# The bias of the last two token tiles moved to ScalarE and GpSimd, and a shorter chain to the integers, in an attention and int8 feed-forward kernel

## The chip, the cores and the metric

The kernel runs on 8 cores of one Trainium2 chip. Each core takes one batch entry (2048 tokens of 1024 features), and nothing passes between cores. The time is device microseconds of the slowest core for one execution. TensorE (PE) multiplies, VectorE (DVE), ScalarE (ACT) and GpSimd (POOL) do the elementwise work, SyncE (SP) issues most of the stores.

## What is computed

```python
s = einsum('bhqd,bhkd->bhqk', q * d**-0.5, k)
attn = where(causal, 1 + s + 0.5*s*s, 0)
o = einsum('bhqk,bhkd->bhqd', attn, v) / (sum(attn) + 1e-6)
x = layernorm(x + (o @ Wo.T))
x_scale = maximum(max|x|, 1e-6) / 127            # per token
x_q = clip(round(x / x_scale), -128, 127)         # int8
y = (x_q @ weight_q.T) * x_scale * weight_scale + bias
out = layernorm(x + y)
```

16 heads of 64; all inputs are float32 but for the int8 weight. The change concerns the lines from the first layernorm to `bias`, for the last 256 of a core's 2048 tokens.

## The kernel before

A core works its 2048 tokens as 16 tiles of 128 tokens (one token per partition). Five attention groups run one after another; projections, output projections and the feed-forward of earlier tiles are woven between the attention's matmuls by a planner in Python (`drive`, with a clock in `at` and `when_idle`). Tiles 0 to 13 pass wholly through that stream. The last two, tiles 14 and 15, form the end of the program (from L1020 on), whose order is written out by hand and which the change alone touches.

Each engine has one queue of instructions, filled in the order in which the helpers are called; an instruction waits for semaphores that other engines raise, and all that is queued behind it on its engine waits too. In the end part `V` puts an instruction on VectorE and `A` one on ScalarE. The order of calls, at the bottom of the function, is:

```python
scales(ta, sums(ta)); tx = sums(tb); turned(ta); hold(4)
scales(tb, tx); biased(ta); forward(ta); turned(tb)
added(ta, 0); added(ta, 1); biased(tb); forward(tb)
tv = spread(ta); added(tb, 0); last_norm(ta, tv)
added(tb, 1); last_norm(tb, spread(tb))
```

with `ta` tile 14 and `tb` tile 15. What each does:

- `sums(t)`: the residual and its sum on VectorE in two halves of 512 columns (L1057), then the sum of squares on ScalarE (L1059).
- `scales(t)`: largest and smallest value (L1068, L1073), the mean and 1/sigma, then a chain of 128x1 VectorE operations, each of which waits for the one before. L1074 and L1075 make the largest deviation `d`, L1077 its scaled form `xs_`, L1078 multiplies `xs_` by 1/127, L1079 takes the reciprocal, L1080 multiplies it by 1/sigma (`s2`), L1081 makes the offset `mm2`. With these ScalarE writes one half of the integers (L1083) and VectorE the other (L1085). A magic constant in float16 rounds them. The stored `xs_` (scale `XS`) is read again by `added`.
- `turned(t)`: eight transposes on TensorE (L1095), copied out of PSUM by ScalarE (L1101) and VectorE (L1104).
- `biased(t)`: x times 1/sigma plus the bias row, 128x1024, one VectorE instruction (L1111). Writing back to the tile's buffer, it waits only for ScalarE's half of the integers.
- `forward(t)`: 16 matmuls of 512 columns into two PSUM banks (L1118).
- `added(t, half)`: VectorE scales one bank (L1129), adds it to the biased x and sums (L1132, which waits for `biased(t)`); ScalarE squares the half and sums (L1136).
- `spread(t)`: mean and variance, on VectorE (L1142, L1143, L1144; L1143 waits for both squares) and a root on ScalarE (L1145).
- `last_norm(t)`: 1/sigma and offset (L1150, L1151), the output in two halves by ScalarE (L1152) and VectorE (L1156), each stored by SyncE.

Elsewhere, L669 is the only other tensor instruction of GpSimd: the division of attention outputs by their sums. L902 is VectorE's final normalization of tiles 0 to 13, and L605 VectorE's first step on the last attention group, after an L669.

Of the kernel before, what the change touches and what calls it, by code (L numbers as in the profile page):

```python
# [10 lines left out]
AF = mybir.ActivationFunctionType  # L11
ALU = mybir.AluOpType
# [24 lines left out]
INV127 = 1.0 / 127.0  # L37
# [80 lines left out]
def build_nc():  # L118
# [17 lines left out]
    P = Prog(nc, ctx)  # L136
# [4 lines left out]
    def sb(name, cols, dt, at=None, parts=128):  # L141
        size = cols * {F32: 4, F16: 2, I8: 1}[dt]
        if at is None:
            at = place[0]
            place[0] += (size + 31) // 32 * 32
        return nc.alloc_sbuf_tensor_at(name, [parts, cols], dt, offset=at)
# [24 lines left out]
    biasb = sb("biasb_sb", D, F32)  # L171
# [31 lines left out]
    tok_c = {}  # L203
# [488 lines left out]
    def home(t):  # L692

        return (x1[t % NX1], t % NX1) if t < NT - 4 else (x1_last[t - NT + 4], NX1 + t - NT + 4)
# [6 lines left out]
    t_xq = {}  # L701
# [6 lines left out]
    t_xb = {}  # L708
# [60 lines left out]
    def chain1(t0, n):  # L769
# [12 lines left out]
        def root():  # L782
            ts = P.op("scalar", lambda e: e.activation(
                V1(a, b), V1(a, b), AF.Sqrt, bias=c_eps), [tv])
            at(1.8, lambda: when_idle(0, lambda: scales(ts, t)))
# [240 lines left out]
    V = lambda fn, w=(): P.op("vector", fn, w)  # L1026
    A = lambda fn, w=(): P.op("scalar", fn, w)
    c1 = lambda f, t: f(t, t + 1)
# [23 lines left out]
    def sums(t):  # L1052
        buf, _ = home(t)
        for half in range(2):
            bk, tok = part[(t, half)]
            xh = buf[:, half * 512:(half + 1) * 512]
            tx = V(lambda e, bk=bk, xh=xh, acc=c1(S1a if half == 0 else S1b, t): e.scalar_tensor_tensor(  # L1057
                xh, bk, 1.0, xh, ALU.mult, ALU.add, accum_out=acc), [tok, t_xl[t]])
        t_junk[0] = t_sq1[t] = A(lambda e: e.activation(  # L1059
            junk[:, :], buf[:, :], AF.Square, scale=1.0 / 32.0, accum_out=c1(SQ, t)), [tx, t_junk[0]])  # L1060
        return tx

    def scales(t, tx):

        buf, _ = home(t)
        m, v, d, mx, mn = c1(M1, t), c1(V1, t), c1(D1, t), c1(MX, t), c1(MN, t)
        xs_, rq, s2, mm2 = c1(XS, t), c1(RQ, t), c1(S2, t), c1(MM2, t)
        V(lambda e: e.reduce_max(mx, buf[:, :], AX.X), [tx])  # L1068
        tm = V(lambda e: e.tensor_scalar(m, c1(S1a, t), c1(S1b, t), -INV1024, ALU.add, ALU.mult), [tx])
        tv = V(lambda e: e.scalar_tensor_tensor(v, m, m, c1(SQ, t), ALU.mult, ALU.subtract),  # L1070
               [tm, t_sq1[t]])
        tv = A(lambda e: e.activation(v, v, AF.Sqrt, bias=c_eps, scale=-1.0), [tv])
        tn = V(lambda e: e.tensor_reduce(mn, buf[:, :], AX.X, ALU.min))  # L1073
        tn = V(lambda e: e.tensor_scalar(mn, mn, m, -1.0, ALU.add, ALU.mult), [tn])  # L1074
        td = V(lambda e: e.scalar_tensor_tensor(d, mx, m, mn, ALU.add, ALU.max), [tn])  # L1075
        tv = V(lambda e: e.reciprocal(v, v), [tv])
        tx = V(lambda e: e.tensor_scalar(xs_, d, v, 1e-6, ALU.mult, ALU.max), [td, tv])  # L1077
        tx = V(lambda e: e.tensor_scalar(xs_, xs_, INV127, None, ALU.mult), [tx])  # L1078
        tx = V(lambda e: e.reciprocal(rq, xs_), [tx])  # L1079
        tx = V(lambda e: e.tensor_tensor(s2, v, rq, ALU.mult), [tx])  # L1080
        tx = V(lambda e: e.tensor_scalar(mm2, m, s2, HMAGIC, ALU.mult, ALU.add), [tx])  # L1081

        ta = A(lambda e: e.activation(  # L1083
            xq[t % 2][:, 0:512], buf[:, 0:512], AF.Identity, bias=mm2, scale=s2), [tx, t_tr.get(t - 2)])
        tb = V(lambda e: e.tensor_scalar(  # L1085
            xq[t % 2][:, 512:1024], buf[:, 512:1024], s2, mm2, ALU.mult, ALU.add), [tx, t_tr.get(t - 2)])
        t_xq[t] = (ta, tb)

    def turned(t):
        got = []  # L1090
        for h in range(2):
            bk, bi, free = take()
            pt = bk.bitcast(F16)
            for j in range(4 * h, 4 * h + 4):
                tok = P.op("tensor", lambda e, j=j, pt=pt: e.transpose(  # L1095
                    pt[:, j * 128:(j + 1) * 128], xq[t % 2][:, j * 128:(j + 1) * 128], ident),
                    [free, t_xq[t][h]] if j % 4 == 0 else [], inc=(j % 4 == 3))
            dst = xqT[t % 2][:, h * 512:(h + 1) * 512]
            src = pt[:, h * 512:(h + 1) * 512]
            if h == 0:  # L1100
                got.append(A(lambda e, dst=dst, src=src: e.activation(dst, src, AF.Copy, bias=-HMAGIC),  # L1101
                             [tok, t_ff.get(t - 2)]))
            else:
                got.append(V(lambda e, dst=dst, src=src: e.tensor_scalar(dst, src, -HMAGIC, None, ALU.add),  # L1104
                             [tok, t_ff.get(t - 2)]))
            bank["free"][bi] = got[h]
        t_xqT[t] = got

    def biased(t):
        buf, _ = home(t)  # L1110
        t_xb[t] = V(lambda e: e.scalar_tensor_tensor(  # L1111
            buf[:, :], buf[:, :], c1(V1, t), biasb[:, :], ALU.mult, ALU.add), [t_xq[t][0], tok_c["biasb"]])

    def forward(t):
        for half in range(2):
# [48 lines left out]
    project(tb, 0, NP)  # L1164
    hold(15)
    scales(ta, sums(ta))
    tx = sums(tb)
    turned(ta)
    hold(4)
    scales(tb, tx)  # L1170
    biased(ta)
    forward(ta)
    turned(tb)
    added(ta, 0)
    added(ta, 1)
    biased(tb)
    forward(tb)
    tv = spread(ta)
# [69 lines left out]
```

How the kernel before makes its waits and increments, by code:

```python
        def play(eng, todo):  # L102
            for waits, fn, sem, k in todo:
                for s, v in waits:
                    eng.wait_ge(s.h, v)
                inst = fn(eng)
                if sem is not None:
                    inst.then_inc(sem.h, k)
```

## Time and profile before

| what | value |
|---|---|
| median of 3 runs | 623.24 us (621.19 to 623.88) |
| profiled execution, its own time | 621.77 us |
| its slowest core (7), first to last instruction | 620.2 us |
| the other cores | 615.7 to 619.9 us |
| mean granted TensorE clock by core | 0.981 to 0.989 of full speed |
| busy on core 7: TensorE | 568.6 us (92%) |
| busy: VectorE / ScalarE / GpSimd | 349.5 us / 369.0 us / 100.1 us |

The profile is of core 7. A timeline row gives the start in us from the span's start, the duration in us, the engine, the line, the operation, output and inputs, the shape, and in brackets how long the engine was idle before it and who released it. Instructions of an engine that follow each other without a wait overlap a little in the rows. The first 583 us of the span lie before the part that is changed.

### The profile page before, as it was taken

The numbers are of one execution on the slowest core, as the hardware profiler recorded it, in microseconds if no ns is written. First come the engines' busy times: TensorE is split into PE (matmuls) and PEld (weight loads), VectorE is DVE, ScalarE is ACT, GpSimd is POOL, SyncE is SP. The second block draws the span as 40 slices with busy tenths as digits, with TensorE's granted clock in tenths as the row PEclk, the third lists the DMA queues.
The fourth block names the chain that finished last, engine by engine and source line by source line (L and its number), as shares of the span: only waits on it lengthen the run. The fifth ranks groups of instructions, "written<-read, shape, count | busy, mean of one in ns | idle before, by whom it ended". The sixth has DMA issues, their size and how long they took to land.

```text
span 620.2 us, 10434 instructions; the slowest of 8 cores (615.7 to 620.2 us)
## 1 busy us (share of the span) xinstructions
PE 568.6 (92%) x3326; PEld 240.5 (39%) x3326; DVE 349.5 (56%) x784; ACT 369.0 (59%) x419; POOL 100.1 (16%) x147
## 2 busy tenths in 40 slices
PE   1899999999988799999998999999999899889982
PEld 0344444443333233333333333344454444444530
DVE  0226456744578667622776755552677744744586
ACT  0000444435557456466777888767889698889433
POOL 9200222125121102232110000111001100000100
PEclk9999999999999899999999999999999999989988
DMA  8999496739822216688220012323001330002201
GB/s 96 160 159 147 68 150 102 141 109 186 214 63 59 44 27 141 153 150 194 46 42 27 27 35 70 109 89 99 27 15 27 107 132 27 15 15 85 90 1 69
DMA packets 34277, 54.54 MB, mean 88 GB/s; under 512 B 10736, under 2 KB 13616, under 8 KB 34224
## 3 DMA queue, kind: packets, MB, share of 16 engines
q0 software_dynamic: 14976, 31.46, 28.5%
q1 hardware_dynamic: 19248, 22.41, 12.3%
q8 instruction: 28, 0.46, 0.3%
q14 instruction: 25, 0.20, 0.1%
HBM read 61.00 MB, written 8.52 MB: 112 GB/s over the span
## 4 chain that ended last, share of the span: by engine, by line
PE 73%; DVE 11%; issue 5%; DMA 4%; ACT 3%; SPq 1%; POOL 0%; DVEq 0%; POOLq 0%; ACTq 0%
PE fb L289 32%; PE oab L577 19%; PE ps L521 13%; PE oab L560 3%; DMA slot<-xT 2%; ACT u L533 2%; PE ps L365 1%; PE ps L289 1%; PE ps L381 1%; DMA zg<-osb 1%; DVE fb L864 1%; PE oab L289 1%; DVE vx L352 1%; DMA rzb<-zscr 1%; PE fb L403 1%
## 5 line engine op out<-in xcount | busy, mean ns | idle before, releaser
L533 ACT ACTIVATE u<-ps,consts 128x1024 f16<-128x1024 f32 (+2 forms) x288 | 303.4, 1067 | 142.3 <-PE ps L521 139.9
L577 PE MATMUL oab<-u,vx 128*128 128x256 f16 (+3 forms) x864 | 171.2, 305 | 0.0
L521 PE MATMUL ps<-qT,kT 64*128 64x256 f16 (+3 forms) x864 | 110.2, 306 | 2.3 <-ACT u L533 2.0
L540 DVE SCALAR_TENSOR_TENSOR u<-u,cst_sb 128x256 f16<-128x256 f16 (+1 forms) x88 | 55.6, 633 | 75.5 <-ACT u L533 75.1
L577 PEld LDWEIGHTS oab<-u,vx 128*128 128x128 f16 x864 | 62.8, 98 | 59.5 <-issue 45.5
L669 POOL TENSOR_TENSOR slot<-osb,rzb 128x512 f16<-128x512 f32 (+1 forms) x35 | 38.8, 1109 | 280.7 <-DMA rzb<-zscr 255.6
L521 PEld LDWEIGHTS ps<-qT,kT 64*128 64x128 f16 x864 | 30.5, 94 | 120.8 <-issue 119.9
L289 PE MATMUL fb<-wf_sb,xqT 128*128 128x512 f16 x224 | 64.3, 394 | 6.6 <-DVE vx L352 3.2
L289 PE MATMUL fb<-slot,wr 128*128 128x512 f16 x256 | 66.8, 379 | 1.7 <-DVE zg L652 0.8
L289 PE MATMUL fb<-wo_sb,slot 128*128 128x512 f16 x224 | 60.7, 379 | 2.0 <-DVE vx L352 1.9
L289 PE MATMUL fb<-wv_sb,slot 128*128 128x512 f16 x192 | 49.1, 379 | 0.8 <-DVE x L868 0.8
L533 ACT ACT_TABLE_LOAD x1 | 1.3, 1283 | 65.0 <-PE ps L521 65.0
L289 PEld LDWEIGHTS fb<-slot,wr 128*128 128x128 f16 x256 | 24.1, 98 | 27.2 <-issue 4.7
L289 PEld LDWEIGHTS fb<-wf_sb,xqT 128*128 128x128 f16 x224 | 21.7, 100 | 23.6 <-issue 9.8
L322 DVE CAST kT<-fb 128x512 f16<-128x512 f32 x26 | 17.9, 688 | 20.6 <-PE fb L289 20.4
L289 PEld LDWEIGHTS fb<-wo_sb,slot 128*128 128x128 f16 x224 | 21.8, 98 | 18.7 <-issue 3.4
L289 PEld LDWEIGHTS fb<-wv_sb,slot 128*128 128x128 f16 x192 | 18.6, 98 | 21.7 <-issue 1.2
L636 DVE COPY osb<-oab 128x512 f32<-128x512 f32 x20 | 13.8, 689 | 21.7 <-PE oab L577 21.7
L365 PE MATMUL ps<-slot,wk_sb 128*128 128x512 f16 x32 | 11.1, 515 | 15.9 <-DMA slot<-xT 15.9
L864 DVE SCALAR_TENSOR_TENSOR fb<-fb,stat,wsb_sb 128x512 f32<-128x512 f32 x28 | 21.1, 754 | 7.8 <-PE fb L289 7.7
L224 POOL DMA_DIRECT2D slot<-xT x16 | 9.1, 619 | 83.3 <-PE ps L521 49.0
L740 DVE SCALAR_TENSOR_TENSOR x<-fb,x 128x512 f32<-128x512 f32 x24 | 16.5, 686 | 10.5 <-PE fb L289 10.5
(183 smaller groups left out, 586.3 us busy)
## 6 DMA issues: line engine op xcount, KB each, us to landing
rzb<-zscr SPq DMA_DIRECT2D x48, 128.0 KB, 3.3
x<-x_tok POOLq DMA_DIRECT2D x12, 512.0 KB, 7.2
out<-x SPq DMA_DIRECT2D x12, 512.0 KB, 3.2
slot<-xT POOLq DMA_DIRECT2D x16, 256.0 KB, 8.1
wr<-wk POOLq DMA_DIRECT2D x16, 256.0 KB, 5.6
wr<-wq POOLq DMA_DIRECT2D x16, 256.0 KB, 6.2
osb<-osb SPq DMA_DIRECT2D x20, 128.0 KB, 2.3
wk_sb<-wk POOLq DMA_DIRECT2D x8, 256.0 KB, 16.6
```

What stands on the lines that cost most here:

```text
L289: tok = P.op("tensor", lambda e, lhs=lhs, rhs=rhs, i=i: e.matmul(out, lhs, rhs, start=(i == 0), stop=(i == n - 1)), list(w) + (list(waits) ...
L322: tok = P.op("vector", lambda e: e.tensor_copy(dst, bk[:, :]), [box[0]])
L365: tok = P.op("tensor", lambda e, fi=fi, p=p, bk=bk: e.matmul(bk, wk[:, p * D + fi * 128: p * D + (fi + 1) * 128], xs(c, fi), start=(fi == ...
L521: tok = P.op("tensor", lambda e, r=r, kt=kt, qo=qo, w=w, col=col, ab=ab: e.matmul(pt[:, ab * 512 + col: ab * 512 + col + w], kT[r:r + 64, ...
L533: tok = P.op("scalar", lambda e: e.activation(dst, src, AF.Square, bias=c_rs, scale=RSQRT2), [t_s[g], t_o.get(g - NU), t_const])
L540: t_u[g] = P.op("vector", lambda e: e.scalar_tensor_tensor(ud, ud, 0.5, tri2[:, None, 0:diag].broadcast_to([128, 2, diag]), ALU.add, ALU.m ...
L560: t_oconst[c] = P.op("tensor", lambda e, ab=ab, base=base: e.matmul(oab[:, at_ab[ab]: at_ab[ab] + width], bs[c % 2][:, base: base + 128], ...
L577: tok = P.op("tensor", lambda e, base=base, qo=qo, w=w, col=col, ab=ab, end=end: e.matmul(oab[:, at_ab[ab] + qo: at_ab[ab] + qo + w], vx[: ...
L636: tb = t_oev[1] = P.op("vector", lambda e: e.tensor_copy(osb[b][:, 512:1024], oab[:, 512:1024]), [tok, before])
L669: t_norm[k] = P.op("gpsimd", lambda e: e.tensor_tensor(slot[o_slot[c]][:, p * 512 + first: p * 512 + first + width], osb[b][:, 0:width], r ...
L740: tok = P.op("vector", lambda e, bk=bk, xh=xh, acc=acc: e.scalar_tensor_tensor(xh, bk, 1.0, xh, ALU.mult, ALU.add, accum_out=acc), [box[0] ...
L864: t1 = P.op("vector", lambda e, bk=bk, half=half: e.scalar_tensor_tensor(bk, bk, XS(t, t + 1), wsb[:, half * 512:(half + 1) * 512], ALU.mu ...
```

## The change

In `scales`, the multiplication of `xs_` by 1/127 leaves the chain: the reciprocal is taken of the larger-valued `xs_`, the factor 127 goes into the next operation, and the stored `xs_` is multiplied by 1/127 behind VectorE's half of the integers. In `biased`, one VectorE instruction becomes a ScalarE multiplication by 1/sigma in place, behind both halves of the integers, and a GpSimd addition of the bias row, behind that.

```diff
-        tx = V(lambda e: e.tensor_scalar(xs_, xs_, INV127, None, ALU.mult), [tx])
-        tx = V(lambda e: e.reciprocal(rq, xs_), [tx])
-        tx = V(lambda e: e.tensor_tensor(s2, v, rq, ALU.mult), [tx])
+        tr = V(lambda e: e.reciprocal(rq, xs_), [tx])
+        tx = V(lambda e: e.tensor_scalar(s2, rq, v, 127.0, ALU.mult, ALU.mult), [tr])
         tx = V(lambda e: e.tensor_scalar(mm2, m, s2, HMAGIC, ALU.mult, ALU.add), [tx])
...
         t_xq[t] = (ta, tb)
+        V(lambda e: e.tensor_scalar(xs_, xs_, INV127, None, ALU.mult), [tr])
...
     def biased(t):
         buf, _ = home(t)
-        t_xb[t] = V(lambda e: e.scalar_tensor_tensor(
-            buf[:, :], buf[:, :], c1(V1, t), biasb[:, :], ALU.mult, ALU.add), [t_xq[t][0], tok_c["biasb"]])
+        tok = A(lambda e: e.activation(buf[:, :], buf[:, :], AF.Copy, scale=c1(V1, t)), list(t_xq[t]))
+        t_xb[t] = P.op("gpsimd", lambda e: e.tensor_tensor(
+            buf[:, :], buf[:, :], biasb[:, :], ALU.add), [tok, tok_c["biasb"]])
```

## Rows read from the trace of the kernel before

**Rows 1.** Windows: us, busy us of each engine (instructions), granted clock, DMA
```profile
610.00:620.00 10.00, 0.00 (x0) 0.00 (x0) 4.95 (x16) 3.55 (x8) 0.00 (x0) 0.71 0.28 106
```

**Rows 2.** Chain that ended last, 603 to 609 us: start, us, what
```profile
603.85 1.07 DVE x1l L1111
...
604.97 0.42 DVE xqT L1104
...
608.50 0.73 ACT junk L1136 x2
```

**Rows 3.** Timeline of VectorE, `scales` of tile 15 and its bias of tile 14
```profile
602.20 0.15 DVE L1078 TENSOR_SCALAR stat<-stat 128x1 f32<-128x1 f32 x1
602.45 0.16 DVE L1079 RECIPROCAL stat<-stat 128x1 f32<-128x1 f32 x1
602.72 0.16 DVE L1080 TENSOR_TENSOR stat<-stat 128x1 f32<-128x1 f32 x1
602.99 0.21 DVE L1081 TENSOR_SCALAR stat<-stat 128x1 f32<-128x1 f32 x1
...
603.77 1.27 DVE L1111 SCALAR_TENSOR_TENSOR x1l<-x1l,stat,biasb_sb 128x1024 f32<-128x1024 f32 x1
```

**Rows 4.** Timeline of TensorE, the transposes and the feed-forward of tile 15
```profile
604.25 0.61 PE L1095 MATMUL ps<-cst_sb,xq 128*128 128x128 f16 x8 [0.53 <-ACT xq L1083]
605.47 3.61 PE L1118 MATMUL oab<-wf_sb,xqT 128*128 128x512 f16 x16 [0.61 <-ACT xqT L1101]
```

**Rows 5.** Timeline of VectorE, 605 to 611 us
```profile
605.31 0.75 DVE L1129 SCALAR_TENSOR_TENSOR ps<-ps,stat,wsb_sb 128x512 f32<-128x512 f32 x1
...
606.17 0.69 DVE L1132 SCALAR_TENSOR_TENSOR x1l<-ps,x1l 128x512 f32<-128x512 f32 x1
...
608.27 0.08 DVE L1132 DVE_READ_ACCUMULATOR x1l<-ps,x1l 128x1 f32 x1
608.27 1.28 DVE L1111 SCALAR_TENSOR_TENSOR x1l<-x1l,stat,biasb_sb 128x1024 f32<-128x1024 f32 x1
...
609.47 0.21 DVE L1142 TENSOR_SCALAR stat<-stat 128x1 f32<-128x1 f32 x1
609.59 0.15 DVE L1143 TENSOR_TENSOR stat<-stat 128x1 f32<-128x1 f32 x1
...
610.85 0.69 DVE L1132 SCALAR_TENSOR_TENSOR x1l<-oab,x1l 128x512 f32<-128x512 f32 x1
```

**Rows 6.** Timeline of ScalarE, 597 to 613 us
```profile
597.89 1.06 ACT L1059 ACTIVATE junk<-x1l 128x1024 int8<-128x1024 f32 x1 [1.11 <-DVE x1l L1057]
598.85 0.19 ACT L1059 ACTIVATION_READ_ACCUMULATOR junk<-x1l 128x1 f32 x1
...
603.29 0.81 ACT L1083 ACTIVATE xq<-x1l,stat 128x512 f16<-128x512 f32 x1 [3.00 <-DVE stat L1081]
604.73 0.60 ACT L1101 ACTIVATE xqT<-ps 128x512 f16<-128x512 f16 x1 [0.62 <-PE ps L1095]
...
608.50 0.63 ACT L1136 ACTIVATE junk<-x1l 128x512 int8<-128x512 f32 x1 [0.76 <-DVE x1l L1132]
609.04 0.19 ACT L1136 ACTIVATION_READ_ACCUMULATOR junk<-x1l 128x1 f32 x1
...
612.33 0.80 ACT L1152 ACTIVATE x1l<-x1l,stat 128x512 f32<-128x512 f32 x1
```

**Rows 7.** Timeline of GpSimd, 407 us and the last two rows it has
```profile
407.70 1.26 POOL L669 TENSOR_TENSOR slot<-osb,rzb 128x512 f16<-128x512 f32 x1 [9.42 <-DMA rzb<-zscr]
...
578.84 1.22 POOL L669 TENSOR_TENSOR slot<-osb,rzb 128x256 f16<-128x256 f32 x1 [12.24 <-DMA rzb<-zscr]
583.72 0.72 POOL L669 TENSOR_TENSOR slot<-osb,rzb 128x256 f16<-128x256 f32 x1 [3.66 <-DMA rzb<-zscr]
```

**Rows 8.** Timeline of VectorE beside the last two GpSimd rows
```profile
578.67 0.81 DVE L902 TENSOR_SCALAR x1l<-x1l,stat 128x1024 f32<-128x1024 f32 x1
...
584.67 0.28 DVE L605 TENSOR_SCALAR rzb<-fb 64x128 f32<-64x128 f32 x1 [1.12 <-POOL slot L669]
```

## Prediction

> **What bounds the kernel now.** TensorE is busy for 92% of the span, but the change does not touch the stretch where that holds. So I read the windows first, to see what is busy at the very end: in the last 10 us TensorE does nothing, while VectorE and ScalarE share the work [rows 1]. Then the chain of waits, to see which of the two carries it. From 589 us on it is VectorE's rows, one behind another, with short excursions to ScalarE. The two bias instructions look alike in the timeline and differ in the chain. The first stands in it [rows 2]. The second does not: there the chain runs over ScalarE's square of tile 14 (L1136), and the bias runs beside it [rows 2, 5]. Last the timelines, engine by engine, to see how much slack each bias has: who waits for it, and how soon. Every microsecond added before the last `added` moves the end, since the stores come after it; an early one has no cushion either.
>
> All starts below are of core 7, before against after. One execution is costed; the same rows on other cores keep the same distances, so I take one delay for all.
>
> **The chain to the integers.** Removed: the step from L1078 to L1079, 602.45 - 602.20 = 0.25 us [rows 3]. The operation that replaces L1080 takes a per-token operand besides a constant, as L1081 does: 0.21 us in place of 0.16, so 0.05 comes back [rows 3]. Net 0.20 us per tile. The multiplication by 1/127 goes behind VectorE's integers, without a wait; a small operation in such a place moves the next by 0.12 (L1142 to L1143) [rows 5]. For tile 14 this hits the two sums of tile 15, but behind them VectorE waits for transposes, which come 0.20 sooner through ScalarE; so both tiles' gains reach tile 15's integers: -0.40 us (bounds -0.2, if the small operation counts fully both times, and -0.5). For tile 15 the operation falls in a wait. Its cover is the transposes: if they were there at once it would cost the 0.12.
>
> **The first bias (tile 14).** Removed from VectorE: 1.27 us, 603.77 to 604.97. What does that free? L1104, next in the queue, needs the transposes: 604.25 + 0.61 = 604.86, and L1104 starts 0.11 later [rows 2, 4]. So the transposes are late next, and removing the bias alone gives nothing. With the 0.40 above they and L1104 come at 604.57, L1129 at 604.91 [rows 2, 5].
>
> Added to ScalarE: a 128x1024 copy with a per-token scale, f32 to f32. It stands behind L1083 of tile 15, which now starts at 603.29 - 0.40 = 602.89. ScalarE rows without a wait overlap by 0.07 to 0.10 (597.89 + 1.06 against 598.85), so the copy starts at 603.63 [rows 6]. No row shows it. From above: 512 columns with per-token scale and offset take 0.80 (L1152), and 512 columns more cost 1.06 - 0.63 = 0.43: 1.23 us. From below: L1101, 512 columns with neither, 0.60 + 0.43 = 1.03. I take 1.20, near L1152, which reads and writes the same tile in the same type [rows 6]. The copy ends at 604.83.
>
> The Trainium skill (VectorE: DVE Perf Modes, the section on the TRN2 errata) gives ScalarE a cost from SBUF to SBUF of 224 cycles plus the columns, at 1.2 GHz: 1.04 us for the copy, an estimate from that page, and by it the whole sum below would be 3.28 us instead of 3.60. The trace agrees where no per-token operand stands (1.06 for L1059) and not where one does: 0.80 for L1152, against 0.61 by the page.
>
> Queued behind the copy on ScalarE: L1101 of tile 15. It starts at about 604.76 against 604.73, so TensorE's feed-forward of tile 15 starts as before, and ends near 609.1; its first reader comes after 611 [rows 4, 6]. This is covered with 2 us to spare.
>
> Added to GpSimd: an add of 128x1024, f32. Its undisturbed rows give 0.72 for 256 columns and 1.26 for 512; 0.54 per 256 more makes 1.26 + 2 x 0.54 = 2.34 us [rows 7]. Those write f16; I know no row with f32, and put 2.1 and 2.9 (the 0.5 us by which the 578.84 row is above its like) as bounds. GpSimd's queue is empty by 584.44. From ScalarE to GpSimd I take 0.16, the distance from VectorE to ScalarE (608.27 + 0.08 to 608.50), and from GpSimd to VectorE 0.23 (583.72 + 0.72 to 584.67) [rows 5 to 8].
>
> Sum: 604.83 + 0.16 + 2.34 + 0.23 = 607.56 for L1132 of tile 14, first half, against 606.17: **+1.39 us**. VectorE idles from 605.66, with the other half's scaling, everything of tile 15, and ScalarE's squares behind it.
>
> **The second bias (tile 15).** From L1132 (606.17) to the end of ScalarE's last square of tile 14 (609.04 + 0.19) it is 3.06 us [rows 5, 6]; nothing in it changes: 610.62. The copy of tile 15 stands behind this square in ScalarE's queue, though its data were ready at 603.7. It starts at 610.52. Then 1.20 + 0.16 + 2.34 + 0.23: L1132 of tile 15, first half, at 614.45 against 610.85, **+3.60 us** in all. Removed from VectorE: 1.28 us at 608.27. That bias covered the squares; without it L1143 waits for them until 610.7, so of the 1.28 only 0.26 would be gained, and it lies before the new wait anyway. Also queued behind the copy is the root of tile 14 (L1145), ready about 612; its reader stands behind L1132, so it costs nothing.
>
> Behind L1132 of tile 15 nothing changes, so the end moves by 3.60: 621.77 + 3.60 = 625.4 for the profiled execution. That execution is 1.5 us under the median of the three runs; the middle of all four times (621.19, 621.77, 623.24, 623.88) is 622.5. I put the prediction on that: **626.1 us**. Bounds for the sum: the copy short twice -0.3, the add short twice -0.5, or long twice +1.1, the chain +0.2: 2.8 to 4.9.
>
> **Rivals.**
>
> *Contention of VectorE and GpSimd.* An L669 of 256 columns took 1.22 us beside L902 and 0.72 alone [rows 7, 8]: some VectorE instructions hold GpSimd up. L1129 of tile 14 (604.91, 0.75 us) meets the start of the first add. If it holds the add until 605.66, that is +0.67: 4.27 in all, 626.8 us. For it speaks the 578.84 row; against it, that L1129 reads PSUM and one SBUF tile and L902 SBUF alone. The second add meets only an idle VectorE. The Trainium skill (SBUF — State Buffer, the section on who interferes with whom) says that a VectorE instruction outside the two-port modes with one SBUF input does not contend, which would leave the sum at 3.60; rows 7 and 8 agree only for the kind that does.
>
> *The waits are partly hidden.* The add is faster than the slope of the f16 rows, or the copy costs no more than a plain one: -0.15 to -0.25 per tile each. Both bounds together give 2.8 us, 625.3 us. It is the same mechanism with a time within 0.5%.
>
> *The bias is off the path.* If copy and add were done before VectorE wants them, only the gains stay: -0.40 for the chain, and -0.26 more where the second bias left the squares uncovered: 621.8 us, no slower. It needs the first copy and add, with both hand-overs, in 606.17 - 0.40 - 603.63 = 2.14 us, where the rows give 3.93; for it speaks only that GpSimd is empty and that rows of GpSimd are rough.
>
> *The shorter chain brings nothing*, if the next operations wait as long as before: +0.40, 4.0 us in all, 626.5 us.
>
> **How the numbers follow.** A measurement of this kernel can tell about 0.5%, 3.1 us, from no change. The forecast at 3.60 is just over that. Chances: forecast with its own spread (3.1 to 4.0) 0.48; contention or a longer add 0.12; the chain brings nothing 0.04; partly hidden, 1.5 to 3.1 us, 0.31; off the path 0.05. So slower 0.63 (the first three, less 0.01), same 0.35, faster 0.02 (no mechanism reaches it; scatter alone). The range goes from 623.9 (1.4 us over 622.5, below the bound of the sum by the scatter of the runs) to 628.2 (4.9 us with the add long, and scatter); it leaves out the off-path case and the tails.
>
> **What would show each step.** The new small step: about 0.9 us from L1077 to the offset, in place of 1.11. The copies: 1.0 to 1.25 us, the second directly behind the square of tile 14. The adds: 2.3 us, the first longer if there is contention. VectorE idle by some 1.9 us before L1132 of tile 14 and 2.6 us before that of tile 15, both released by GpSimd. The last square, root and outputs at the old distances. The prediction is wrong if L1132 waits for nothing, if the adds take under 1.5 us, or if the two copies do not stand where ScalarE's queue puts them.

## The result, and the profile after

| what | before | after |
|---|---|---|
| median of 19 runs | 622.73 us | 625.54 us |
| ratio, 95% interval | | 1.004 (1.0029 to 1.0052) |
| profiled execution: span of the slowest core | 620.2 us (core 7) | 623.9 us (core 2) |
| VectorE busy / instructions on it | 349.5 us / 784 | 345.0 us / 782 |

The medians count every execution; the ratios, here and below, leave out those in which the cores of one die or both ran at a lower clock and took some per cent longer. The kernel became slower by 0.4%: 2.8 us by the medians, 2.5 us (1.8 to 3.2) by the ratio. The forecast was 626.1 us, in a range of 623.9 to 628.2.

Cores reach the end part at different times, so spans compare badly. A better ruler for all that follows is **the tail**: from the start of the first residual sum of tile 14 (L1057) to the start of the last sum of tile 15 (L1132 before, L1133 after). Both instructions are VectorE's and are in every kernel. Read on all 8 cores:

```
kernel   tail of cores 0 to 7, us
before   23.52 23.86 23.52 23.51 23.56 23.52 23.90 23.70
after    26.83 26.82 26.82 26.82 26.81 26.82 26.82 26.81
```

The new tail repeats within 0.02 us. From the last sum to the end of the span it is 7.1 to 7.5 us before and 7.1 to 7.8 us after, the same instructions in both and then the landing of the last stores; the last output of ScalarE ends 3.97 to 4.00 us after the start of that sum on every core of every kernel here. So on an undisturbed core the change costs 26.82 - 23.52 = 3.30 us. Why three cores had a longer tail before comes with experiments 9 and 10.

The page of the changed kernel, its engines:

```profile
PE 567.0 (91%) x3326; PEld 239.7 (38%) x3326; DVE 345.0 (55%) x782; ACT 370.9 (59%) x421; POOL 105.1 (17%) x149
```

Timeline of VectorE after, core 2, the end of `scales` of tile 15 and what follows. It answers to [rows 3] and [rows 5].

```profile
602.41 0.16 DVE L1078 RECIPROCAL stat<-stat 128x1 f32<-128x1 f32 x1
602.68 0.21 DVE L1079 TENSOR_SCALAR stat<-stat 128x1 f32<-128x1 f32 x1
603.00 0.21 DVE L1080 TENSOR_SCALAR stat<-stat 128x1 f32<-128x1 f32 x1
603.32 0.55 DVE L1084 TENSOR_SCALAR xq<-x1l,stat 128x512 f16<-128x512 f32 x1
603.78 0.15 DVE L1087 TENSOR_SCALAR stat<-stat 128x1 f32<-128x1 f32 x1
604.98 0.42 DVE L1104 TENSOR_SCALAR xqT<-ps 128x512 f16<-128x512 f16 x1 [1.05 <-PE ps L1095]
605.33 0.75 DVE L1130 SCALAR_TENSOR_TENSOR ps<-ps,stat,wsb_sb 128x512 f32<-128x512 f32 x1
607.82 0.69 DVE L1133 SCALAR_TENSOR_TENSOR x1l<-ps,x1l 128x512 f32<-128x512 f32 x1 [1.75 <-POOL x1l L1112]
...
610.97 0.16 DVE L1144 TENSOR_TENSOR stat<-stat 128x1 f32<-128x1 f32 x1 [0.65 <-ACT junk L1137]
...
614.50 0.69 DVE L1133 SCALAR_TENSOR_TENSOR x1l<-oab,x1l 128x512 f32<-128x512 f32 x1 [2.38 <-POOL x1l L1112]
```

VectorE now idles where the bias stood: 1.05 us for the transposes, 1.75 us and 2.38 us for GpSimd, 0.65 us for the square that the second bias had covered.

The two other engines after, core 2 (timeline of ScalarE and GpSimd), to be set beside [rows 6] and [rows 7]:

```profile
603.31 0.81 ACT L1082 ACTIVATE xq<-x1l,stat 128x512 f16<-128x512 f32 x1 [2.79 <-DVE stat L1080]
...
604.03 1.13 ACT L1111 ACTIVATE x1l<-x1l,stat 128x1024 f32<-128x1024 f32 x1
...
605.07 0.57 ACT L1101 ACTIVATE xqT<-ps 128x512 f16<-128x512 f16 x1
...
605.37 2.34 POOL L1112 TENSOR_TENSOR x1l<-x1l,biasb_sb 128x1024 f32<-128x1024 f32 x1 [18.91 <-ACT x1l L1111]
...
610.69 0.19 ACT L1137 ACTIVATION_READ_ACCUMULATOR junk<-x1l 128x1 f32 x1
610.78 1.13 ACT L1111 ACTIVATE x1l<-x1l,stat 128x1024 f32<-128x1024 f32 x1
...
612.05 2.34 POOL L1112 TENSOR_TENSOR x1l<-x1l,biasb_sb 128x1024 f32<-128x1024 f32 x1 [4.34 <-ACT x1l L1111]
```

The second copy starts at the moment the square of tile 14 is read out, 610.78, though its input was ready at 604.12. The chain of waits says the same in its own way. In [rows 2] VectorE's bias and later ScalarE's square stood there; now it is twice a relay over three engines:

```profile
604.03 1.14 ACT x1l L1111
...
605.37 2.35 POOL x1l L1112
...
607.82 0.70 DVE x1l L1133 x2
...
610.15 0.72 ACT junk L1137 x2
610.87 1.05 ACT x1l L1111
...
612.03 2.38 POOLq L110
```

### The profile page after: what moved, and what is told of

It is laid out like the page before. It is cut to its first block, busy times and chain, and to the rows that moved or that the text cites. A ratio compares the mean times of both kernels' runs of the same rounds, so it can differ in the third digit from the quotient of the medians.

```text
span 623.9 us, 10439 instructions; the slowest of 8 cores (619.4 to 623.9 us)
## 1 busy us (share of the span) xinstructions
PE 567.0 (91%) x3326; PEld 239.7 (38%) x3326; DVE 345.0 (55%) x782; ACT 370.9 (59%) x421; POOL 105.1 (17%) x149
## 4 chain that ended last, share of the span: by engine, by line
PE 76%; DVE 8%; DMA 5%; issue 4%; ACT 4%; POOL 2%; POOLq 0%; DVEq 0%; ACTq 0%
PE fb L289 34%; PE oab L577 21%; PE ps L521 14%; DMA wv_sb<-wv 5%; PE oab L560 3%; ACT u L533 2%; PE ps L289 1%; POOL wk_sb L231 1%; DVE fb L864 1%; PE fb L823 1%; PE oab L381 1%; PE fb L403 1%; PE fb L381 1%; PE fb L585 1%; DVE vx L352 0%
## 5 line engine op out<-in xcount | busy, mean ns | idle before, releaser
L540 DVE SCALAR_TENSOR_TENSOR u<-u,cst_sb 128x256 f16<-128x256 f16 (+1 forms) x88 | 53.6, 610 | 76.4 <-ACT u L533 76.0
L669 POOL TENSOR_TENSOR slot<-osb,rzb 128x512 f16<-128x512 f32 (+1 forms) x35 | 38.9, 1111 | 290.1 <-DMA rzb<-zscr 280.3
L289 PE MATMUL fb<-wo_sb,slot 128*128 128x512 f16 x224 | 62.1, 386 | 2.0 <-DVE vx L352 1.9
L365 PE MATMUL ps<-slot,wk_sb 128*128 128x512 f16 x32 | 9.2, 438 | 15.5 <-DMA slot<-xT 15.5
```

What stands on the lines that cost most here:

```text
L289: tok = P.op("tensor", lambda e, lhs=lhs, rhs=rhs, i=i: e.matmul(out, lhs, rhs, start=(i == 0), stop=(i == n - 1)), list(w) + (list(waits) ...
L540: t_u[g] = P.op("vector", lambda e: e.scalar_tensor_tensor(ud, ud, 0.5, tri2[:, None, 0:diag].broadcast_to([128, 2, diag]), ALU.add, ALU.m ...
L669: t_norm[k] = P.op("gpsimd", lambda e: e.tensor_tensor(slot[o_slot[c]][:, p * 512 + first: p * 512 + first + width], osb[b][:, 0:width], r ...
```

## The experiments

The theory: copy and add stand in series with VectorE, and the second pair starts late because of its place in ScalarE's queue. The rivals: VectorE's own time sets the end, or contention, that is, GpSimd and VectorE holding each other up; the chain and the bias interact.

Each diff is against the changed kernel, where nothing else is said.

**1. The chain alone.**

```diff
-        tok = A(lambda e: e.activation(buf[:, :], buf[:, :], AF.Copy, scale=c1(V1, t)), list(t_xq[t]))
-        t_xb[t] = P.op("gpsimd", lambda e: e.tensor_tensor(
-            buf[:, :], buf[:, :], biasb[:, :], ALU.add), [tok, tok_c["biasb"]])
+        t_xb[t] = V(lambda e: e.scalar_tensor_tensor(
+            buf[:, :], buf[:, :], c1(V1, t), biasb[:, :], ALU.mult, ALU.add), [t_xq[t][0], tok_c["biasb"]])
```

> Only the shorter chain and the moved 1/127 multiplication; both biases stay one VectorE instruction. Measure: the tail, from the start of the first residual sum of tile 14 (L1057) to the start of the last sum of tile 15 (L1132). Before it is 23.52 us on the cores where TensorE's clock stays full there, after 26.82. My theory (chain gain and bias waits are independent, and the waits carry the loss): tail 23.24, that is -0.28, execution about -0.3 us. Rival (the shorter chain gives nothing or costs by the moved operation): tail 23.5 to 23.6.

Measured: tail 23.22 to 23.24 on all 8 cores, -0.29 against the undisturbed cores. Medians 622.56 against 623.26 us, ratio 0.9988 (0.9976 to 1.0001), which alone would not tell it from nothing. By the tail the shorter chain is a gain.

**2. The bias alone.**

```diff
-        tr = V(lambda e: e.reciprocal(rq, xs_), [tx])
-        tx = V(lambda e: e.tensor_scalar(s2, rq, v, 127.0, ALU.mult, ALU.mult), [tr])
+        tx = V(lambda e: e.tensor_scalar(xs_, xs_, INV127, None, ALU.mult), [tx])
+        tx = V(lambda e: e.reciprocal(rq, xs_), [tx])
+        tx = V(lambda e: e.tensor_tensor(s2, v, rq, ALU.mult), [tx])
...
-        V(lambda e: e.tensor_scalar(xs_, xs_, INV127, None, ALU.mult), [tr])
```

> Only the biases on ScalarE and GpSimd; the chain as before. My theory: the whole loss is here, tail 26.82 + 0.34 = 27.16 us, execution about +3.6 us against before. Rival (chain and bias interact, for instance the small operation behind the integers delays the copy): tail near 26.8 to 26.9 or over 27.4.

Measured: tail 27.14 to 27.22 on seven cores and 27.36 on core 1, medians 626.04 against 623.26, ratio 1.0046 (1.0029 to 1.0063). The bias is the whole loss, +3.64. With the chain's -0.29 that makes 3.35, and the change itself 3.30. The 0.05 between them is about the 0.06 by which the moved small operation pushes the bias of tile 14 on VectorE in experiment 1; in the changed kernel it falls in a wait there.

**3. The second bias earlier in the queues.**

```diff
     turned(tb)
+    biased(tb)
     added(ta, 0)
     added(ta, 1)
-    biased(tb)
```

> As the changed kernel, but the bias of tile 15 is put into the queues right behind its transposes, ahead of the sums and squares of tile 14. My theory (the second wait is the place of the copy in ScalarE's queue, not the length of copy and add): the second add follows the first on GpSimd and ends before VectorE wants it, the wait before the sum of tile 15 goes, tail 26.82 - 2.26 = 24.56 us, execution about +1.0 us against before. Rival (the add's length or contention of two adds and VectorE sets it): the sum of tile 15 still waits over 1 us for GpSimd, tail over 25.5.

Measured: tail 24.62 to 24.64 on all cores, medians 623.49 against 623.26, ratio 1.0005 (0.9992 to 1.0019). Moving one call gives back 2.19 of the 3.30 us with the same instructions and lengths. The timeline of core 2 of this kernel:

```profile
601.25 4.66 POOL L1112 TENSOR_TENSOR x1l<-x1l,biasb_sb 128x1024 f32<-128x1024 f32 x2 [21.36 <-ACT x1l L1111]
601.43 1.13 ACT L1111 ACTIVATE x1l<-x1l,stat 128x1024 f32<-128x1024 f32 x1
...
603.72 0.69 DVE L1133 SCALAR_TENSOR_TENSOR x1l<-ps,x1l 128x512 f32<-128x512 f32 x1 [1.75 <-POOL x1l L1112]
...
607.27 0.75 DVE L1130 SCALAR_TENSOR_TENSOR oab<-oab,stat,wsb_sb 128x512 f32<-128x512 f32 x1
608.20 0.69 DVE L1133 SCALAR_TENSOR_TENSOR x1l<-oab,x1l 128x512 f32<-128x512 f32 x1 [0.18 <-DVE oab L1130]
```

Both adds run one behind the other (4.66 us for two) and end at 605.9; the sum of tile 15 at 608.20 waits for VectorE's own L1130 alone. The second wait was the place, not the length. The first, 1.75 us, stays. Of the 0.07 over the expectation 0.06 is in the last two rows: the sum starts 0.93 after L1130 in place of 0.87. This sum is the first that waits for the second add as well as for L1130; that this is the cause is inferred, not tested.

**4. Each bias in halves.**

```diff
-        tok = A(lambda e: e.activation(buf[:, :], buf[:, :], AF.Copy, scale=c1(V1, t)), list(t_xq[t]))
-        t_xb[t] = P.op("gpsimd", lambda e: e.tensor_tensor(
-            buf[:, :], buf[:, :], biasb[:, :], ALU.add), [tok, tok_c["biasb"]])
+        toks = [A(lambda e, a=a: e.activation(
+            buf[:, a:a + 512], buf[:, a:a + 512], AF.Copy, scale=c1(V1, t)), list(t_xq[t])) for a in (0, 512)]
+        t_xb[t] = [P.op("gpsimd", lambda e, a=a: e.tensor_tensor(
+            buf[:, a:a + 512], buf[:, a:a + 512], biasb[:, a:a + 512], ALU.add),
+            [toks[a // 512], tok_c["biasb"]]) for a in (0, 512)]
...
-            [t1, t_xb[t]])
+            [t1, t_xb[t][half]])
```

> As the changed kernel, but each bias in two halves of 512 columns on both engines, and each sum waits for its own half alone. My theory (a chain of latencies, copy then add then sum): copy 0.70, add 1.26 us each; first wait shorter by 1.52, second by the same again, tail 26.82 - 3.03 = 23.79 us, execution about +0.3 us against before. Rival (GpSimd costs mostly per instruction, or the two engines disturb each other in one tile): halves take over 1.6 us each, tail over 24.8.

Measured: tail 24.03 to 24.05, medians 623.27 against 623.26, ratio 1.0002 (0.9985 to 1.002). Timeline of core 2, each row two instructions:

```profile
597.55 1.32 ACT L1111 ACTIVATE x1l<-x1l,stat 128x512 f32<-128x512 f32 x2
...
598.46 2.50 POOL L1113 TENSOR_TENSOR x1l<-x1l,biasb_sb 128x512 f32<-128x512 f32 x2 [20.28 <-ACT x1l L1111]
...
599.84 0.69 DVE L1135 SCALAR_TENSOR_TENSOR x1l<-ps,x1l 128x512 f32<-128x512 f32 x1 [0.24 <-POOL x1l L1113]
```

Two halves take 2.50 us against 2.34 for the whole, so nearly all of GpSimd's cost is by the element, and a second instruction costs 0.16 us more. The first wait shrinks from 1.75 to 0.24 us, the second from 2.38 to 0.88. The tail is 0.25 over the expectation. Most of it is in small delays on VectorE: two sums start 0.92 and 0.93 behind the operation before them in place of 0.87, as in experiment 3, and from the first sum of tile 15 to its second scaling, with the small operations of `last_norm` between, it is 1.51 us in place of 1.41. The cause of these delays was not tested.

**5. The first bias back on VectorE, the second off it and early.**

```diff
+        if t == NT - 2:
+            t_xb[t] = V(lambda e: e.scalar_tensor_tensor(
+                buf[:, :], buf[:, :], c1(V1, t), biasb[:, :], ALU.mult, ALU.add), [t_xq[t][0], tok_c["biasb"]])
+            return
...
     turned(tb)
+    biased(tb)
     added(ta, 0)
     added(ta, 1)
-    biased(tb)
```

> Chain as changed, the bias of tile 14 again one VectorE instruction, that of tile 15 on ScalarE and GpSimd right behind its transposes. My theory (the first bias fits into VectorE's wait for the transposes, the second into the slack of the two other engines): tail 23.23 - 0.26 = 22.97 us, up to 23.06 with the 0.06 to 0.09 that a wait on a further engine costs; execution -0.5 us against before. Rival (GpSimd's add beside VectorE's sums slows them or comes late): tail over 23.3.

Measured: tail 23.03 to 23.05, medians 622.76 against 623.32, ratio 0.9985 (0.997 to 0.9999). No wait for GpSimd is left.

**6. As 5, with the order of the sums changed.** The diff is against the kernel of experiment 5.

```diff
     forward(tb)
-    tv = spread(ta)
-    added(tb, 0)
-    last_norm(ta, tv)
+    added(tb, 0)
+    tv = spread(ta)
     added(tb, 1)
+    last_norm(ta, tv)
     last_norm(tb, spread(tb))
```

> As e5_first_on_vector, and the first scaling and sum of tile 15 are put ahead of the mean and variance of tile 14, the normalization of tile 14 behind the last sum of tile 15. My theory (with the bias off VectorE, the sums of tile 15 can run where VectorE waited for squares): tail 23.23 - 1.98 = 21.25, up to 21.45 with extra waits; from the last sum to the end 0.1 to 0.2 us more; execution about -2.1 us against before, ratio 0.9966. Rival (the add of tile 15 is then needed at the moment it ends, or later: 0.2 us of slack by my sum): VectorE waits for GpSimd, tail 21.6 or more.

Measured: tail 21.30 to 21.31 on all cores, medians 621.41 against 623.32, ratio 0.9965 (0.9948 to 0.9982): faster than both kernels. The normalization of tile 14 now stands behind the last sum, outside the tail, but it falls in waits there: the last output of ScalarE still ends 3.97 or 3.98 us after that sum's start, and the runs, 0.35% faster, bear the tail out. Timeline of core 2:

```profile
607.27 2.35 POOL L1116 TENSOR_TENSOR x1l<-x1l,biasb_sb 128x1024 f32<-128x1024 f32 x1 [21.34 <-ACT x1l L1115]
...
609.02 0.76 DVE L1134 SCALAR_TENSOR_TENSOR oab<-oab,stat,wsb_sb 128x512 f32<-128x512 f32 x1
...
609.96 0.69 DVE L1137 SCALAR_TENSOR_TENSOR x1l<-oab,x1l 128x512 f32<-128x512 f32 x1 [0.18 <-DVE oab L1134]
```

The add ends at 609.62, before VectorE wants it at 609.9. It took 2.35 us beside VectorE's sums and scalings, which read PSUM and one SBUF tile, and 2.34 beside an idle VectorE (the second add of the changed kernel).

**7. The order of 6 with both biases on VectorE.** The diff is against the kernel of experiment 1, in which each bias is one VectorE instruction.

```diff
     biased(tb)
     forward(tb)
-    tv = spread(ta)
     added(tb, 0)
-    last_norm(ta, tv)
+    tv = spread(ta)
     added(tb, 1)
+    last_norm(ta, tv)
     last_norm(tb, spread(tb))
```

> The reordering of e6_reordered with both biases one VectorE instruction each. My theory: only the normalization of tile 14 leaves the way (0.80 us), the second bias stays in it: tail 23.23 - 0.80 = 22.43 us, so that the move of the second bias is worth 1.2 us once the order is changed. Rival (the order alone does it): tail below 21.6.

Measured: tail 22.43 to 22.45, medians 622.04 against 623.32, ratio 0.9974 (0.9956 to 0.9993). The move of the second bias is worth 22.44 - 21.31 = 1.13 us in this order, and 23.23 - 23.04 = 0.19 us in the old one (experiments 1 and 5). The order alone, with both biases on VectorE, is worth 23.23 - 22.44 = 0.79 us. What an instruction's removal brings depends on what else can use its place.

**8. No bias at all.** This kernel leaves out the multiplication by 1/sigma and the bias of the two tiles.

```diff
-        tok = A(lambda e: e.activation(buf[:, :], buf[:, :], AF.Copy, scale=c1(V1, t)), list(t_xq[t]))
-        t_xb[t] = P.op("gpsimd", lambda e: e.tensor_tensor(
-            buf[:, :], buf[:, :], biasb[:, :], ALU.add), [tok, tok_c["biasb"]])
+        t_xb[t] = t_xq[t][0]
```

> As the changed kernel with the multiplication by 1/sigma and the bias left out for tiles 14 and 15: the most that taking them off VectorE can bring. My theory (the first bias lies wholly beside the transposes, the second all but 0.26 us beside ScalarE's squares): tail 23.23 - 0.06 - 0.26 = 22.91 us. Rival (VectorE's own time is the bound there): tail 23.23 - 1.08 - 1.20 = 20.95 us.

Measured: tail 22.91 to 22.93 on all cores. It ran once, in 623.77 us; the kernel before has a median of 623.32, and single executions scatter by more than the effect. Taking 2.55 us of bias off VectorE, with no work in its place, brings 0.31 us in the old order. That was all there was to win on the biases without a change of order.

**9 and 10. TensorE's idle stretch and its clock.** The three long tails of before asked for this. In the kernel before, four filler matmuls behind the transposes of tile 14 took 1.03 us on three cores and 1.85 to 1.91 on five. Core 1 of before, timeline of TensorE:

```profile
596.41 0.54 PE L1095 MATMUL oab<-cst_sb,xq 128*128 128x128 f16 x4 [2.04 <-ACT xq L1083]
596.74 0.63 PE L1095 MATMUL fb<-cst_sb,xq 128*128 128x128 f16 x4
597.17 1.91 PE L1048 MATMUL fb<-cst_sb 128*128 128x512 f16 x4
```

Its granted clock in the windows around it (columns as in [rows 1]):

```profile
590.00:595.00 5.00, 4.36 (x21) 1.76 (x18) 4.07 (x13) 1.44 (x3) 0.00 (x0) 1.00 0.01 3
595.00:597.00 2.00, 0.59 (x7) 0.62 (x8) 1.78 (x6) 0.81 (x1) 0.00 (x0) 0.87 0.00 0
597.00:599.00 2.00, 2.00 (x8) 0.62 (x6) 1.74 (x5) 1.63 (x3) 0.00 (x0) 0.50 0.00 0
```

A granted clock of 0.50 is the lower of its two levels, 1.2 GHz. TensorE had stood idle for 2.04 us. With the shorter chain that stretch is 1.84 or 1.85 us (0.74 on core 7 of the changed kernel), and none of the 64 core traces with it (the changed kernel and experiments 1 and 3 to 8) showed the fall; of the 16 with the old chain (before and experiment 2) 8 did.

Experiment 9, against the kernel before:

```diff
-    hold(15)
+    hold(16)
```

> The kernel before with one filler matmul more (16 in place of 15) ahead of the transposes of tile 14, so that TensorE sits idle there for about 1.83 us in place of 2.05, as with the shorter chain. In the traces so far the four filler matmuls behind those transposes took 1.03 us on all 64 cores with the shorter chain and 1.85 to 1.91 us on 8 of 16 cores with the old chain. Theory (the idle stretch of TensorE decides whether its clock falls): 1.03 us on all 8 cores, tail 23.52 on all. Rival (chance, or another part of the chain): 1.85 to 1.91 on some cores again.

Experiment 10, against the kernel of experiment 1:

```diff
-    hold(15)
+    hold(14)
```

> The kernel with only the shorter chain and one filler matmul less (14), so that TensorE sits idle for about 2.06 us, as before the change. Theory (the idle stretch decides): 1.85 to 1.91 us for the four filler matmuls on several cores, and tails up to 0.3 us over 23.23 on them. Rival (chance, or another part of the chain): 1.03 us on all cores.

Measured, with one execution each, on another chip than experiments 1 to 8 (622.52 and 625.07 us; the kernel before took 622.83 there): with 16 fillers the stretch was 1.82 to 1.84 us, the four fillers took 1.03 on all cores and the tail was 23.52 or 23.53 on all. With 14 it was 2.06 us; the four took 1.82, 1.91 and 1.88 on three cores, 1.23 and 1.26 on two more, and 1.03 on three. So the expectation of experiment 9 came true, and that of experiment 10 for the falls but not for their price: on the cores with 1.23 and 1.26 the tail became 24.97 and 24.94 us, 1.7 us over the others, where at most 0.3 was expected. Core 1 of this kernel, TensorE's timeline:

```profile
598.89 1.23 PE L1048 MATMUL fb<-cst_sb 128*128 128x512 f16 x4
601.25 6.15 PE L1118 MATMUL ps<-wf_sb,xqT 128*128 128x512 f16 x16 [1.14 <-ACT xqT L1101]
607.23 0.61 PE L1095 MATMUL ps<-cst_sb,xq 128*128 128x128 f16 x8
```

Here the clock fell later: it is 1.00 up to 599 us and 0.50 from 601 to 605. Most of the feed-forward of tile 14 ran at the lower level, 6.15 us against 3.61. The transposes of tile 15 stand behind it, and VectorE waited.

What a fall costs depends on where it lands. In the kernel before, the first four transposes of tile 14 took 0.54 and 0.57 us on cores 1 and 6, in place of 0.38, and their tails are 0.34 and 0.38 us longer. On core 7 only the last four were slowed (0.59 in place of 0.39): 0.18 us. On core 0 the clock fell behind the transposes and the tail is 23.52, no longer at all. Seven of the 13 falls in these traces cost 0.06 us or less.

## Why the prediction was right

Point by point, with its own terms, on undisturbed cores:

| term | predicted | measured |
|---|---|---|
| chain to the integers, both tiles | -0.40 | -0.34 |
| copy on ScalarE | 1.20 | 1.13, twice |
| add on GpSimd | 2.34 | 2.34, twice |
| ScalarE to GpSimd | 0.16 | 0.21 and 0.14 |
| GpSimd to VectorE | 0.23 | 0.11, twice |
| whole | +3.60 | +3.30 |

- *What bounds it.* Right: VectorE's rows carry the chain, but transposes and squares are close behind, and of 2.55 us of bias in it 0.31 could be won (experiment 8; by the prediction 0 for the first, 0.26 for the second, and the 0.06 of the moved small operation, which then falls in a wait).
- *The chain.* The step is 0.20 us shorter, as worked out. The 0.06 that is missing is the moved operation in tile 14. The prediction let it hide behind the wait for the transposes. On the cores where TensorE's clock stays full there is no such wait, L1104 following the sums at once. The wait was read on core 7, where the clock had fallen, and the sentence that the same rows on other cores keep the same distances was wrong: the tails before range from 23.51 to 23.90 us. Where the small operation counts, it counts 0.06 (596.78 to 596.84 on core 2), not 0.12.
- *The first wait.* Right in kind and place. The copy begins where ScalarE's queue puts it, and L1101 behind it is covered.
- *The second wait.* Right, and shown by experiment 3: 2.19 us of the loss is the copy's place behind the squares.
- *The size.* The mis-sized term is the hand-over from GpSimd to VectorE, 0.23 predicted and 0.11 measured: 0.24 us in both tiles. The copy is the other: 0.07 twice. By 3.60 - 0.24 - 0.14 + 0.03 + 0.06 the sum gives 3.31.
- *Where the 0.23 came from.* It was read from L605, which waits for GpSimd's L669 and for TensorE's L585 (last row on core 7: 583.87 + 0.27). On all eight cores of before L605 starts 0.53 or 0.54 us after L585 ends. From the end of L669 it is 0.23 on core 7 and 0.54 to 1.17 on the others. So L605 went by TensorE on core 7 too, though the timeline names GpSimd, and the row held no hand-over from GpSimd.
- *The core.* The 3.31 is for an undisturbed core, but the sum was made for core 7, and there the change costs 26.81 - 23.70 = 3.11: the shorter chain also took away the 0.18 of the fallen clock, a term that the prediction did not have.
- *Smaller readings.* The add came out at 2.34 as worked out from rows that write f16; the prediction could not know that writing f32 would cost no more. The 0.16 from VectorE to ScalarE is 0.15 by its rows.
- *The Trainium skill's rule for ScalarE.* By the page VectorE: DVE Perf Modes (the TRN2 errata) the copy was estimated at 1.04 us. The trace has 1.13, between that and the 1.20 of the sum.
- *Contention.* Did not occur. L1130 started at 605.33, the add at 605.37, and they took 0.75 and 2.34 us; the second add, beside an idle VectorE, took 2.34 as well. This agrees with the Trainium skill (SBUF — State Buffer, who interferes with whom) for a VectorE operation with a single SBUF input outside the two-port modes.
- *Slower by over 0.5%.* That chance was the largest at 0.63, and the measured 0.4% falls on the other side of the bound. It missed the 3.1 us by 0.3 by the medians and by 0.6 by the ratio, whose interval takes in the bound. The sum was near the bound, and the bounds on its terms leaned upward.
- *From the tail to the runs.* The tail says 3.30 us, the runs 2.5 or 2.8. Part of the distance is that some cores of before carried 0.2 to 0.4 us of the fallen clock, which the shorter chain takes away: against cores 1 and 6 the change costs 2.96 and 2.92 us. In the runs of experiments 1 to 4 the mean span of the eight cores moved by -0.28, +3.73, +1.00 and +0.46 us against the kernel before, each to about 0.4, beside -0.29, +3.64, +1.11 and +0.52 in the tail. So the tail holds for the mean core. The slowest core alone moved by -0.55, +3.27, +0.59 and +0.09, each time 0.3 to 0.5 us lower. The four share the same runs of before, and this may be the scatter of those; it stays open.

## What to carry to other kernels

Work taken off a busy engine brings only as much as the next late input allows: read for each instruction who would be late next. When work goes to two other engines in series, put its call where its input is ready, not where the old one stood, since it inherits the place in their queues as well. Then change the order on the relieved engine; the move alone was worth 0.19 us here, and with the new order 1.13 us.

## What was not expected of the hardware

- **A shorter chain on VectorE kept TensorE's clock up.** With TensorE idle for 2.04 to 2.07 us before the transposes, its clock fell to the lower level on 13 of 24 core traces; with 1.85 us or less on none of 72. Experiments 9 and 10 brought about each case once. One filler matmul of 0.22 us more or less moved a kernel from one case to the other. A fall cost from nothing to 0.4 us, and twice 1.7 us, by where it landed.
- **A per-token scale costs ScalarE less than scale and offset together.** The copy of 1024 columns with a scale took 1.13 us. From 512 columns with both (0.80) and 0.43 for 512 more one would come to 1.23, an estimate. In experiment 4 two instructions of 512 columns with a scale took 1.32 together, under twice 0.80.
- **A sum on VectorE starts 0.06 us later** behind its own predecessor (0.93 in place of 0.87) in the kernels where it is the first to wait for a GpSimd add too, though that add had ended 0.3 us before or more.
